# Ten slots for gathered rows, halved row buffers, and the softmax division on the finished attention row

## The reference

```python
nk = flatK[:, :, idx_table]          # 12 rows of keys for each of the 512 rows
nv = flatV[:, :, idx_table]
self_logits = jnp.einsum('bhnd,bhnd->bhn', Q, K) * scale
nbr_logits = jnp.einsum('bhld,bhlnd->bhln', Q, nk) * scale
all_logits = jnp.concatenate([self_logits[..., None], nbr_logits], axis=-1)
w = jax.nn.softmax(all_logits, axis=-1)
all_v = jnp.concatenate([V[:, :, :, None, :], nv], axis=3)
out = jnp.einsum('bhln,bhlnd->bhld', w, all_v)
x = _layernorm(x + out @ Wo.T + bo)
x = _layernorm(x + relu(x @ w1 + b1) @ w2 + b2)
```

## Time and profile before

| | before |
|---|---|
| runs | 2362.0, 2362.91, 2380.96 us; median 2362.91 |
| profiled execution: own time, span | 2362.72 us, 2360.7 us |
| PE, DVE busy | 2049.5 us, 1616.1 us |
| ACT, POOL busy | 1072.2 us, 1036.9 us |
| mean granted clock of PE | 0.957 |

### The profile page before, as it was taken

How to read it: one execution, slowest core, us unless ns; L and a number is a source line. 1 busy time by engine, 2 the same in 40 slices (tenths; PEclk the granted TensorE clock), 3 DMA queues, 4 the chain that set the end, 5 groups by cost and what they waited for, 6 DMA issues and landing times.

```text
span 2360.7 us, 33037 instructions
## 1 busy us (share of the span) xinstructions
PE 2049.5 (87%) x11360; PEld 1023.6 (43%) x11360; DVE 1616.1 (68%) x2129; ACT 1072.2 (45%) x1854; POOL 1036.9 (44%) x1084
## 2 busy tenths in 40 slices
PE   4899999999999999996147888998989999988997
PEld 2333333333333333331014555555555555555555
DVE  8564647566564647552568888888888888888850
ACT  3354545455555545464013444444444444444444
POOL 3232534244352535233444464465555555455420
PEclk9999999999999999998568999999999999999999
DMA  5442434434342434331875675665665675675520
GB/s 193 146 126 73 144 97 131 145 108 152 121 149 79 142 96 130 117 108 63 311 268 186 220 235 188 220 231 199 221 236 195 215 255 195 206 249 195 199 85 18
DMA packets 188800, 392.40 MB, mean 166 GB/s; under 512 B 20692, under 2 KB 82260, under 8 KB 188632
## 3 DMA queue, kind: packets, MB, share of 16 engines
q1 hardware_dynamic: 133336, 188.91, 25.1%
q0 software_dynamic: 55296, 201.35, 24.6%
HBM read 312.33 MB, written 77.59 MB: 165 GB/s over the span
## 4 chain that ended last, share of the span: by engine, by line
DVE 28%; DMA 11%; POOL 5%; issue 4%; PE 3%; ACT 0%; DVEq 0%; SPq 0%; ACTq 0%; POOLq 0%
DMA nb<-kv_flat,idx_rows 10%; DVE bank L1497 10%; DVE logits L1444 5%; POOL nb L1568 5%; DVE nb L1493 5%; DVE nb L1435 4%; PE bank L1172 1%; PE bank L1148 1%; DMA own<-kv_flat 1%; DVE bank L1503 1%; DVE logits L1448 1%; DVE own L1439 1%; DVE total L1474 1%; DVE top L1466 1%; DVE weights L1481 0%
## 5 line engine op out<-in xcount | busy, mean ns | idle before, releaser
L712 DVE TENSOR_REDUCE neg_max<-rows_ps 128x2 f32<-128x1024 f32 x256 | 312.4, 1220 | 298.3 <-PE rows_ps L499 298.2
L1568 POOL DMA_INDIRECT nb<-kv_flat,idx_rows x384 | 366.6, 955 | 138.0 <-issue 86.2
L1435 DVE TENSOR_TENSOR nb<-nb,bank 128x1024 f32<-128x1024 f32 x192 | 231.7, 1218 | 142.5 <-DMA nb<-kv_flat,idx_rows 137.7
L627 ACT ACTIVATE probsT<-e_ps 128x1024 f32<-128x1024 f32 x256 | 262.0, 1023 | 145.1 <-PE e_ps L527 144.8
L1596 POOL TENSOR_TENSOR nb<-nb,weights 128x1024 f32<-128x1024 f32 x96 | 182.5, 1914 | 281.8 <-DVE weights L1481 281.1
L1497 DVE TENSOR_TENSOR bank<-bank,nb 128x512 f32<-128x512 f32 x384 | 268.2, 698 | 24.7 <-DVE bank L1497 0.5
L1148 PE MATMUL bank<-x2T_hi,w_hi_sb 128*128 128x256 f16 x1024 | 282.4, 276 | 0.7 <-issue 0.7
L1148 PE MATMUL bank<-x2T_lo,w_hi_sb 128*128 128x256 f16 x1024 | 281.9, 275 | 0.0
L1148 PE MATMUL bank<-x2T_hi,w_lo_sb 128*128 128x256 f16 x1024 | 281.4, 275 | 0.0
L517 PE MATMUL o_ps<-probsT,v_sb 128*33 128x512 f32 x1024 | 269.6, 605 | 6.3 <-ACT oT L624 6.1
L1444 DVE TENSOR_REDUCE logits<-nb 128x32 f32<-128x1024 f32 x192 | 230.0, 1211 | 0.0
(11 more groups left out here) (158 smaller groups left out, 3611.8 us busy)
## 6 DMA issues: line engine op xcount, KB each, us to landing
kv_flat<-kv_nat SPq DMA_DIRECT2D x128, 256.0 KB, 3.3
own<-kv_flat SPq DMA_DIRECT2D x32, 512.0 KB, 3.8
q_stack<-qk_dram SPq DMA_DIRECT2D x96, 128.0 KB, 3.0
k_stack<-qk_dram SPq DMA_DIRECT2D x96, 128.0 KB, 3.3
piece<-in_pieces SPq DMA_DIRECT2D x40, 256.0 KB, 3.5
in_sb<-in_xT SPq DMA_DIRECT2D x8, 1024.0 KB, 6.6
in_sb<-in_ctxT SPq DMA_DIRECT2D x8, 1024.0 KB, 5.6
qk_dram<-hi SPq DMA_DIRECT2D x32, 256.0 KB, 2.2
```

The lines of the kernel that those rows point to most:

```text
L627: act.activation(probsT[:, (d - E_LAG) % TT, :, :], e_ps[:], ACT.Exp, scale=1.0 / (Q_UP * K_UP))\
L712: dve.tensor_reduce(neg_max[:, g % 2, at:at + 2], rows_ps[:], AX.X, ALU.max, negate=True).then_inc(max_done, 1)
L1435: dve.tensor_tensor(kk, kk, q.unsqueeze(1).to_broadcast([P, GN, D]), ALU.mult)\
L1568: pool.indirect_dma_start(nb[:, slot(lt, g), k, :], None, kv_flat, bass.IndirectOffsetOnAxis(idx_rows[:, lt, at:at + 1], 0))\
```

## The change

nb gets ten slots. The room comes from buffers with half the slots: o_sb and x2 hold one tile and y_sb one round; the small bias buffers of the start lie in y_sb and x2T. With one slot each, the accumulator copy waits for the store of the round before, and the store stands earlier in SP's order. Slot numbers count over the whole batch loop, since 24 groups a batch are no multiple of ten.

The weights are no longer divided by their total. ACT copies the exponentials into PSUM for DVE (where the query was); the total and its reciprocal come behind the first value product, and a last product of DVE writes O times the reciprocal to o_sb, in place of ACT's copy.

```diff
-SLOTS = 8
+SLOTS = 10
...
-            o_sb = sb("o_sb", [P, 2, D])
+            o_sb = sb("o_sb", [P, D])
...
-            x2 = sb("x2", [P, 2, D])
-            squares = sb("squares", [P, 1 + RT, D], F16)
-            y_sb = sb("y_sb", [P, TT, D])
+            x2 = sb("x2", [P, D])
+            squares = sb("squares", [P, 2, D], F16)
+            y_sb = sb("y_sb", [P, RT, D])
...
+            bias_in, bias_hi, bias_lo = y_sb[0:2], x2T_hi[0:2, 0:2, :], x2T_lo[0:2, 0:2, :]
...
-            def slot(lt, g):
-
-                return (lt * NG + g) % SLOTS
+            def slot(b, lt, g):
+
+                return ((b * TT + lt) * NG + g) % SLOTS
 
             def fills(b, lt, g):
 
-                return b * (TT * NG // SLOTS) + (lt * NG + g) // SLOTS + 1
+                return ((b * TT + lt) * NG + g) // SLOTS + 1
...
                     if ahead > 0:
                         load_own(nb_, nh * RT)
+                    if not (isinstance(b, int) and b * 2 + half < 2):
+                        store(b - 1, half)
                     if ahead > 1:
                         load_x1(fb, fh * RT + 1)
                     if ahead > 0:
                         load_res(nb_, nh * RT)
                         load_own(nb_, nh * RT + 1)
-                    if not (isinstance(b, int) and b * 2 + half < 2):
-                        store(b - 1, half)
...
-                def copy_o(b, lt):
-
-                    act.wait_ge(o_part, START + (b * TT + lt + 1) * O_STEPS)
-                    act.activation(o_sb[:, lt % 2, :], O[:], ACT.Copy).then_inc(o_copied, 1)
-
                 def exponentials(b, lt):
...
                         .then_inc(exp_done, 1)
+                    act.wait_ge(exp_done, START + b * TT + lt + 1)
+                    act.activation(Q[lt % RT][:, 0:(NN + 1) * H], weights[:].rearrange("p n h -> p (n h)"), ACT.Copy)\
+                        .then_inc(weights_ready, 1)
...
                 def copy_acc(b, half):
 
                     act.wait_ge(mlp_ready, START + b * 2 + half + 1)
-                    act.wait_ge(out_stored[half], START + b * (16 * RT))
+                    pb, ph = last_round(b, half)
+                    if b * 2 + half:
+                        act.wait_ge(out_stored[ph], START + (pb + 1) * (16 * RT))
...
                 def y_square(b, half):
                     act.wait_ge(y_centre, START + b * 2 + half + 1)
-                    act.wait_ge(y_squared, START + (b * 2 + half) * RT)
                     for lt in tiles(half):
                         s = 2 + lt % 2
+                        act.wait_ge(y_squared, START + (b * 2 + half) * RT + lt % RT)
...
-                        if attend and c + 1 == OUT_AT[0]:
-                            copy_o(ab, first)
-                        if attend and c + 1 == OUT_AT[1]:
-                            copy_o(ab, second)
...
-                def normalise(b, lt):
+                def totals(b, lt):
                     n = b * TT + lt
                     dve.wait_ge(exp_done, START + n + 1)
                     dve.tensor_reduce(total[:], weights[:].rearrange("p n h -> p h n"), AX.X, ALU.add)\
                         .then_inc(norm_step, 1)
-                    dve.wait_ge(norm_step, START + n * 3 + 1)
+                    dve.wait_ge(norm_step, START + n * 2 + 1)
                     dve.reciprocal(total[:], total[:]).then_inc(norm_step, 1)
-                    dve.wait_ge(norm_step, START + n * 3 + 2)
-                    shares = total[:].unsqueeze(1).to_broadcast([P, NN + 1, H])
-                    dve.tensor_tensor(weights_ps(lt), weights[:], shares, ALU.mult).then_inc(norm_step, 1)
-                    dve.tensor_tensor(weights[:], weights[:], shares, ALU.mult).then_inc(weights_ready, 1)
 
                 def values(b, lt):
...
-                    dve.wait_ge(norm_step, START + n * 3 + 3)
+                    dve.wait_ge(weights_ready, START + n + 1)
...
                     multiply(0)
+                    totals(b, lt)
...
                         accumulate(g, 1)
+                    dve.wait_ge(norm_step, START + n * 2 + 2)
+                    dve.wait_ge(o_part, START + (n + 1) * O_STEPS)
+                    if n:
+                        dve.wait_ge(turn_ready, START + turn_of(*last_tile(b, lt), "o") + 1)
+                    dve.tensor_tensor(o_sb[:].rearrange("p (h d) -> p h d", h=H), O[:].rearrange("p (h d) -> p h d", h=H),
+                                      total[:].unsqueeze(2).to_broadcast([P, H, DH]), ALU.mult).then_inc(o_copied, 1)
...
-                        normalise(b, lt)
                         values(b, lt)
```

More of the change, by code:

```diff
@@ L1024, in store @@
                         sp.dma_start(out[bass.ds(b, 1), lt * P:(lt + 1) * P, :].rearrange("a p d -> p (a d)"),
-                                     y_sb[:, lt, :]).then_inc(out_stored[half], 16)
+                                     y_sb[:, lt % RT, :]).then_inc(out_stored[half], 16)
                 def round_moves(b, half, ahead):
@@ L1113, in turn_out @@
                     pe.wait_ge(o_copied, START + b * TT + lt + 1)
[L1114 removed]
+                    turn(turn_of(b, lt, "o"), o_sb[:])
                 def turn_query(b, lt):
@@ L1294, in x2_sum @@
                     act.wait_ge(proj_ready, START + n + 1)
-                    act.activation(x2[:, s, :], PROJ[:], ACT.Copy, scale=1.0 / W_UP, accum_out=sums[:, s:s + 1])\
+                    act.activation(x2[:], PROJ[:], ACT.Copy, scale=1.0 / W_UP, accum_out=sums[:, s:s + 1])\
                         .then_inc(x2_summed, 1)
@@ L1304, in x2_square @@
                     act.wait_ge(x2_squared, START + n)
-                    act.activation(squares[:, 0, :], x2[:, s, :], ACT.Square, bias=neg_mean[:, s:s + 1],
+                    act.activation(squares[:, 0, :], x2[:], ACT.Square, bias=neg_mean[:, s:s + 1],
                                    accum_out=sum_squares[:, s:s + 1]).then_inc(x2_squared, 1)
@@ L1326, in y_square @@
                     act.wait_ge(y_centre, START + b * 2 + half + 1)
-                    act.wait_ge(y_squared, START + (b * 2 + half) * RT)
                     for lt in tiles(half):
                         s = 2 + lt % 2
-                        act.activation(squares[:, 1 + lt % RT, :], y_sb[:, lt, :], ACT.Square, bias=neg_mean[:, s:s + 1],
+                        act.wait_ge(y_squared, START + (b * 2 + half) * RT + lt % RT)
+                        act.activation(squares[:, 1, :], y_sb[:, lt % RT, :], ACT.Square, bias=neg_mean[:, s:s + 1],
                                        accum_out=sum_squares[:, s:s + 1]).then_inc(y_squared, 1)
@@ L1336, in y_apply @@
                         s = 2 + lt % 2
-                        act.activation(y_sb[:, lt, :], y_sb[:, lt, :], ACT.Identity, scale=rstd[:, s:s + 1],
+                        act.activation(y_sb[:, lt % RT, :], y_sb[:, lt % RT, :], ACT.Identity, scale=rstd[:, s:s + 1],
                                        bias=shift_by[:, s:s + 1]).then_inc(y_ready, 1)
@@ L1432, in multiply @@
                         if g < NG:
-                            dve.wait_ge(gathered[slot(lt, g)], (16 * GN) * fills(b, lt, g))
-                            kk = nb[:, slot(lt, g), :, 0:D]
+                            dve.wait_ge(gathered[slot(b, lt, g)], (16 * GN) * fills(b, lt, g))
+                            kk = nb[:, slot(b, lt, g), :, 0:D]
                             dve.tensor_tensor(kk, kk, q.unsqueeze(1).to_broadcast([P, GN, D]), ALU.mult)\
@@ L1567, in gather @@
                         at = g * GN + k
-                        pool.indirect_dma_start(nb[:, slot(lt, g), k, :], None, kv_flat,
+                        pool.indirect_dma_start(nb[:, slot(b, lt, g), k, :], None, kv_flat,
                                                 bass.IndirectOffsetOnAxis(idx_rows[:, lt, at:at + 1], 0))\
-                            .then_inc(gathered[slot(lt, g)], 16)
+                            .then_inc(gathered[slot(b, lt, g)], 16)
                 def summed(b, i):
@@ L1592, in weight_values @@
                     for g in groups:
-                        pool.wait_ge(gathered[slot(lt, g)], (16 * GN) * fills(b, lt, g))
-                        vv = nb[:, slot(lt, g), :, D:2 * D].rearrange("p n (h d) -> p n h d", h=H)
+                        pool.wait_ge(gathered[slot(b, lt, g)], (16 * GN) * fills(b, lt, g))
+                        vv = nb[:, slot(b, lt, g), :, D:2 * D].rearrange("p n (h d) -> p n h d", h=H)
                         w = weights[:, g * GN:(g + 1) * GN, :].unsqueeze(3).to_broadcast([P, GN, H, DH])
```

29 lines of the change are left out of this document (12 added, 17 removed).

## The result

The changed kernel took 2474.74 us (median of 4 runs, 2464.6 to 2478.01) against 2362.45 beside it: a ratio of 1.0455, 95% interval 1.0388 to 1.0523. I had forecast 2263. The profiled execution took 2464.6 us for a span of 2462.6.

The account below looks back on a forecast made before the run. PE was taken to bound the second stage at 62.9 us a round: 14 rounds plus a 32.7 us leg make 913.3 against 1015.7, -102.4, with +2.7 at the start; 2362.7-99.7 = 2263 us, range 2245 to 2310.

Parts of the forecast that it names:

- The gather waits: DVE's waits for gathered rows in the steady part, 4.35 us a tile, were taken as gone with ten slots.
- The division: On DVE, two products of the old division go and one final product comes: net +0.14 us a tile.
- The final product: DVE's new 128x512 product from PSUM into o_sb, priced at 0.72 us (bounds 0.6 and 0.8).
- The wait for the weights: DVE's wait for ACT's exponentials and their copy, put at 0.4 to 0.5 us once a round.
- the loop: PE's transposes, ACT's weights and DVE's row tied together: 62.3 us a round, 0.6 below PE's.
- PE's round: PE's two legs between transposes of o_sb, 32.7 and 30.2 us: 62.9 us a round at full clock.
- the two short waits for hid_hi and hid_lo: PE's waits for ACT, 0.65 and 0.56 us each, taken as unchanged within PE's second leg.
- The clock: PE was taken at full clock in the steady part, since no long wait would be left.
- Halved buffers: Three added waits from o_sb, x2 and y_sb with fewer slots, taken as costing 0.
- The start: Twenty gathers at once delay tile 1's own row by 5.4 us; +1.0 us net, plus 1.7 for a cold first leg.
- The slower one: Rival: short PE waits at each transpose keep its clock low, at 0.85 74.0 us a round, 2420 us; chance 0.03.
- The range: From DVE's own pace with no start cost, 2245 us, to the half-gather-wait rival with its unknowns, 2310 us.

Follow-up runs that it names:

- e10: The changed kernel with each tile's last two gather groups issued after x2's standard deviation, cutting POOL's row of twelve calls into eight and four; 2250.85 us.
- e3: The kernel before with the halved buffers and SP's new order alone (eight slots, old division); 2361.29 us, ratio 1.0007.
- e12: The changed kernel in its own order with four small dummy POOL operations between the sixth and seventh gather call; 2253.64 us.
- e14: The changed kernel with five gather groups ahead of x2's standard deviation and one behind it; 2252.53 us.
- e11: The changed kernel with three gather groups ahead of x2's standard deviation and three behind it; 2523.23 us, ratio 1.0691.
- e16: e10 run again in a set with the unchanged changed kernel; 2305.69 us, ratio 0.9712.
- e8: The kernel before, unchanged, run once more for a second trace; 2363.53 us.
- e17: Second run of the kernel before with SP storing the previous round ahead of a load of x1; 2364.92 us, ratio 0.9995.

## Why the prediction was wrong

**The gather waits: right.** None is left in the changed kernel's steady part, and at e10's round of 62.4 us, where there is less time for them, one of 0.7 us.

**The division: the product right, the net wrong in sign.** The final product takes 0.692 us (forecast 0.72). For DVE the forecast was a net loss of 0.14 us a tile, 4 us in all where DVE sets the pace; measured is a gain, 7 to 11 us at eight slots and 7 to 10 at ten. Why, no run shows. The wait for the weights was forecast at 0.5 us every second tile and is 4.6 (45.8 us, 10 times), because ACT is late; in e10 it comes once in the whole stage, 2.1 us, so even there the loop was not as forecast (DVE waits for the next query's projection instead, 14.9 us, 12 times).

**PE's round: the step that failed.** It said that PE is bound at 62.9 us, "with the two short waits for hid_hi and hid_lo in it ..., which the change leaves alone", and that what is queued behind ACT's copy is needed later, "so beside PE it costs nothing". The sum came out where signals are prompt, in e10, which differs from the changed kernel only in POOL's order: 62.4 us a round, 903.6 from tile 2 to tile 31 (913.3 forecast), 2250.85 in all. What failed is the hand-over from PE to ACT, the time from the end of a product to the start of the ACT instruction that waits for it: the prediction put it at nothing beyond the old waits, and so took every signal to be prompt, since the trace of the kernel before has no late one. In the changed kernel's first run and in four sets of six PE's signals came 3 to 8 us late among the gathers. PE's waits for hid_lo, forecast at 0.56 us, became up to 5.5, and the round 77.0.

Why the same lateness costs 0 at eight slots and 15 us a round at ten: a round of 70 us holds 7.1 us in which PE is idle anyway, 4.8 of them for o_sb, and the ten slots take most of those. Where it falls counts too. In e3 the transposes of o_sb come 3.7 us after the row of calls begins (1721.12 against 1717.46), ACT's copies of them get through, and PE has the 12 products of project_out to do while ACT stands. In the changed kernel they come 5.9 us after it (1728.55 against 1722.68), the copies fall among the late signals, and PE stands. That is read from these rows; no run moved the transposes alone.

**The clock.** Behind waits of 0.7 us it stays at 1.00 (e10: no longer wait within the rounds, 1.00 over the steady part), as the earlier trace rows had it. The Trainium skill's rule on short idle times, page "TensorE: Matmul & The Clock Gate", section "A second HAM failure mode: psum-queue depth-cycling", would have kept a slow stretch each round; the trace does not bear it out. In the changed kernel the clock falls, behind waits of 5 us, and that is 4.3 of the 14.7 us.

**Halved buffers: right,** 1.0007 [0.9997, 1.0016].

**The start.** The wait for tile 1's own row ends at 1211.94, forecast 1212:

```profile
1211.94 0.69 DVE L1431 TENSOR_TENSOR own<-own,bank 128x512 f32<-128x512 f32 x1 [18.34 <-DMA own<-kv_flat]
```

**The rivals.** The slower one had the clock at 0.85 through many short waits of PE in near balance. The sign was its, and a part of the mechanism (0.91), but the waits are long, come from ACT, and make two thirds of the loss by themselves (4.6 of 6.9 us a round against the kernel before).

**The range.** Its lower end was added up wrongly: 896 us in place of 1015.7 gives 2243, not 2245. Nothing hangs on it.

**The fastest version** that leaves nothing out can't be told between e10, e12 and e14, whose ratios of 0.9527 to 0.9537 overlap. e10 alone is measured in both conditions: 2250.85 us where signals are prompt, 2305.69 where they are late, faster than the kernel before in both (0.9537 and 0.9712), and than the changed kernel where the two stood side by side.

## What to carry to other kernels

Slack that a forecast takes away may be paying for something the trace does not show, so a change that leaves an engine with no slack needs the longest hand-over it can meet, not the one of a single trace: look at a second trace, from another chip and another time, before pricing a hand-over at nothing. Work that is not due soon (here the gathers for the tile after next) need not be issued in one unbroken row: the order with its last four calls moved behind other work was 161 us faster where signals were late, and at 2250.85 us nothing shows that it costs anything where they are prompt. Not every cut is safe: one group more behind it made e11 the slowest kernel of all. And kernels that are to be compared belong in the same set: six of my runs told a clean story that the next three took apart.

## What was not expected of the hardware

A product's signal reached ACT and SP 3 to 8 us after its recorded end, during a row of POOL's gather calls or up to 2.3 us behind its last one, whatever the bytes of a call (4096 or 2048 a row). The same program may show it in one set and not in another (e10 and e16: 2250.85 and 2305.69 us, 0 and 85.8 us of "remote"), and kernels with slack take the same time either way (e8, and e17 with SP's early store: 2363.53 and 2364.92 us).
